# A recurrent layer's second-half products and output product taken from fp16 and bf16 parts

## The reference

```
y  = layer_norm(x)
xi = y @ w_ih.T + b_ih                       # 768 gates' inputs per token
for each token:                              # 512 steps, one after the other
    r = sigmoid(xi_r + h @ w_hr.T + b_hr)    # h: 256 numbers for each sequence
    z = sigmoid(xi_z + h @ w_hz.T + b_hz)
    n = tanh(xi_n + r * (h @ w_hn.T + b_hn))
    h = (1 - z) * n + z * h
x  = x + norm(norm(x) + h @ w_out.T + b_out)         # "first sum"
xf = norm(x)
e  = argmax(xf @ gate_W.T + gate_b)                  # one of 8 experts per token
m  = relu(xf @ wi_W.T + wi_b + (xf @ lora_A[e].T) @ lora_B[e].T)   # 512 hidden
x  = x + norm(m @ wo_W.T + wo_b)                     # "second sum"
```

## Time and profile before

| | |
|---|---|
| median of 3 runs | 1976.41 us (1976.2 to 1980.02) |
| the profiled execution | 1975.0 us |
| its span, first to last instruction | 1973.1 us |
| TensorE busy, products | 1683.9 us (85%) |
| VectorE busy | 1177.6 us (60%) |
| ScalarE busy | 739.8 us (37%) |
| first block, ahead of the recurrence | 0 to 33.9 us |
| its two writes of `Y1` and of `Y2`, 512 elements each | 2.6 us each (L361, L436) |
| `HS` from `HR` by DMA | 128 times 32 KB, 1.7 us from issue to landing |

### The profile page before, as it was taken

How to read it: one execution, slowest core, us unless ns; L and a number is a source line. 1 busy time by engine, 2 the same in 40 slices (tenths; PEclk the granted TensorE clock), 3 DMA queues, 4 the chain that set the end, 5 groups by cost and what they waited for, 6 DMA issues and landing times. The chain is left out here.

```text
span 1973.1 us, 68602 instructions
## 1 busy us (share of the span) xinstructions
PE 1683.9 (85%) x27122; PEld 1261.1 (64%) x27137; DVE 1177.6 (60%) x5580; ACT 739.8 (37%) x2556; POOL 362.9 (18%) x597
## 2 busy tenths in 40 slices
PE   4888878999999999999999988348988889897857
PEld 3676767888888888888888866224545455444423
DVE  5666666665655665556556544436676566675366
ACT  2333332222222222222222222014665566665645
POOL 2010100000000000000000012362123313411244
PEclk9999999999999999999999999977999899998979
DMA  5000000000000000000000000076436625732001
GB/s 121 7 8 7 7 7 7 5 3 4 3 5 5 4 4 3 4 3 4 3 4 3 4 1 0 2 118 99 60 54 91 99 25 79 101 56 28 1 6 38
DMA packets 80562, 53.56 MB, mean 27 GB/s; under 512 B 28558, under 2 KB 80166, under 8 KB 80422
## 3 DMA queue, kind: packets, MB, share of 16 engines
q1 hardware_dynamic: 78566, 51.54, 16.5%
q10 hardware_dynamic: 1856, 0.07, 0.1%
HBM read 31.84 MB, written 15.47 MB: 24 GB/s over the span
## 5 line engine op out<-in xcount | busy, mean ns | idle before, releaser
L653 PEld LDWEIGHTS PS<-G,W 128*128 128x128 f16 x18432 | 548.4, 105 | 181.2 <-DVE G L896 164.4
L653 PE MATMUL PS<-G,W 128*128 128x8 f16 x18432 | 577.7, 168 | 89.3 <-DVE G L896 85.5
L1700 DVE TENSOR_REDUCE MX<-PS 128x1 f32<-128x512 f32 (+3 forms) x352 | 223.0, 636 | 191.9 <-PE PS L1447 182.5
L805 ACT ACTIVATE tr<-PS 128x16 f32<-128x16 f32 x512 | 96.3, 188 | 578.3 <-PE PS L653 578.3
L1603 ACT ACTIVATE PT<-PS 128x512 f32<-128x512 f32 (+1 forms) x352 | 193.8, 559 | 171.0 <-PE PS L1463 167.1
L882 DVE SCALAR_TENSOR_TENSOR u_<-tr,PS 128x16 f32<-128x16 f32 x512 | 89.1, 174 | 274.7 <-PE PS L653 253.5
L666 PE MATMUL PS<-Y,V 128*128 (+1 forms) x2322 | 175.3, 192 | 0.0
L807 ACT ACTIVATE tz<-PS 128x16 f32<-128x16 f32 x512 | 93.7, 183 | 189.9 <-PE PS L653 189.9
L1444 PE MATMUL PS<-KS,QS 99*128 99x256 bf16 (+3 forms) x512 | 136.6, 319 | 31.6 <-DMA KS<-k_parts 20.7
L615 POOL TENSOR_TENSOR rt<-mv,eps 128x1 f32<-128x1 f32 x96 | 18.2, 189 | 746.9 <-DVE mv L917 746.9
L661 PE MATMUL PS<-ones,brow 3*128 3x32 bf16 x1032 | 141.0, 195 | 4.8 <-PEq L185 3.9
(11 more groups left out here) (324 smaller groups left out, 2677.4 us busy)
## 6 DMA issues: line engine op xcount, KB each, us to landing
QS<-q_parts SPq DMA_DIRECT2D x48, 256.0 KB
KS<-k_parts SPq DMA_DIRECT2D x48, 256.0 KB
q_parts<-PQ SPq DMA_DIRECT2D x16, 384.0 KB, 12.8
k_parts<-PK SPq DMA_DIRECT2D x16, 384.0 KB, 13.1
HS<-HR SPq DMA_DIRECT2D x128, 32.0 KB, 1.7
X<-in_L_attn_x_dram SPq DMA_DIRECT2D x4, 512.0 KB, 8.8
out_dram<-X SPq DMA_DIRECT2D x8, 256.0 KB, 2.3
s_hh<-in_L_attn_w_hh_dram SPq DMA_DIRECT2D x1, 768.0 KB, 5.5
```

Of the source, the lines that this page charges most:

```text
L653: return pe.matmul(bank[:, p, o:o + B], W[:, kc, w:w + P], G[:, kc, :], start=False, stop=True, skip_group_check=True)
L805: act.activation(tr[:, :], pR[:, p, o:o + NSTEP], ACT.Tanh, scale=gate_scale).then_inc(hn_tr.sem, 1)
L1700: dve.tensor_reduce(MX[:, g % 2, heads[0]:heads[-1] + 1, NT - 1 - it], p_x[:, k % 2, 0:len(heads) * w].rearrange("p (a w) -> p a w", w=w), ...
```

## The change

- All fp32 products of the units become sums of products of 16-bit parts. `w_out`, the gate weights, `wi` and `wo` are scaled by powers of two and split into high and low fp16 (`OU`, `GA`, `WI`, `DN`) during the preparation of sequences 3 to 6. `p_gy`, `p_ga`, the `wi` product and `p_dn` are three fp16 products each (`TERMS`) where one fp32 product was.
- `lora_B` is split into three bf16 parts; `LB` holds four of them stacked on 128 rows and `LB2` two on 64 rows. The masked `ML` is split and repeated in `MP` (two operations at s = 15, two in the next unit's s = 0), turned by two bf16 transposes (s = 1) and copied to `LAT` and `LAT2` (s = 2). The bias of the hidden layer is a 3-row product `wibr`.
- `p_base` takes one whole PSUM bank; per chunk it is one 3-row product, three 128-row products, one 128-row product with `LB` and one 64-row product with `LB2`. Chunks 0 and 1 are made at s = 3, chunks 2 and 3 at s = 4. One relu of 512 elements (s = 5) writes the high part `IH`; VectorE makes the low part `IL` in two halves of 256 (s = 6, 7); `p_dn` follows at s = 8 and 9, `T2` at 10, moments at 11 and 12, `N2` and the sum at 14.
- `XFT` becomes `XH` (ScalarE) and `XL` (VectorE), both at s = 11.
- The states are stored as parts: `GB` replaces `G1` and `G2`, the DMA copies `GB` to an fp16 `HS`, `HB` is two copies of 256 elements. `HR` stays for the step. The wait for the DMA moves ahead of the high part's write.
- `Y1` and `Y2` have the token innermost. So the gates' values in PSUM lie in the order chunk, sequence, step: the 16 values of a step are 16 bytes apart, and each product writes 8 columns at that distance.

The diff, cut to its core:

```diff
-        Y1 = sb(gru_scope, "Y1", [P, S + U, B], FP16)
-        HS = sb(gru_scope, "HS", [P, S, HC, B])
+        Y1 = sb(gru_scope, "Y1", [P, B, S + U], FP16)
+        HS = sb(gru_scope, "HS", [P, S // U, 2, U, NSTEP], FP16)
...
+            GB = sb(ctx, "GB", [P, 2, 2, U, NSTEP], FP16)
...
-                        sp.dma_start(HS[:, bass.ds(at, U)]..., HR[:, p])
+                        sp.wait_ge(g2_ready.sem, ...)
+                        sp.dma_start(HS[:, bass.ds(sp.snap(q * 2 + p), 1)]..., GB[:, p])
...
-                    o = NSTEP * k + B * mc
-                    return pe.matmul(bank[:, p, o:o + B], W[:, kc, w:w + P], G[:, kc, :],
+                    at = mc * U * B
+                    state = GB[:, p, part, k - 1, :] if k else GB[:, 1 - p, part, U - 1, :]
+                    return pe.matmul(bank[:, p, at:at + U * B].rearrange("p (b u) -> p b u", u=U)[:, :, k], W[:, kc, w:w + P],
+                                     state[:, kc * B:(kc + 1) * B], ...)
...
-                                    pe.matmul(o, V[:, w], Y[:, rows, :].rearrange("p s b -> p (s b)"),
+                                    pe.matmul(o, V[:, w], Y[:, :, rows],
...
+                TERMS = ((0, 0), (0, 1), (1, 0))
...
+                    if s == 12:
+                        for h, w in TERMS:
+                            last = pe.matmul(p_ga, (XH, XL)[h][:, :], GA[w][:, :], ...)
...
+                    if s == 1:
+                        pe.wait_ge(mlp.sem, mlp.value(pe, u))
+                        pe.transpose(p_laT[:, 0:P], MP[:, 0:4, :]..., identb[:, :])
+                        pe.transpose(p_laT[0:2 * E * R, P:2 * P], MP[:, 4:6, :]..., identb[:, :])
+                    for c in {3: (0, 1), 4: (2, 3)}.get(s, ()):
+                        at, o = slice(c * P, (c + 1) * P), p_base[:, c * P:(c + 1) * P]
+                        pe.matmul(o, wibr[:, at], ones3w[:, :], start=(c == 0), ...)
+                        for h, w in TERMS:
+                            pe.matmul(o, WI[w][:, at], (XH, XL)[h][:, :], ...)
+                        pe.matmul(o, LB[:, at], LAT[:, :], ...)
+                        last = pe.matmul(o, LB2[:, at], LAT2[:, :], ...)
+                    for c in {8: (0, 1), 9: (2, 3)}.get(s, ()):
+                        for h, w in TERMS:
+                            last = pe.matmul(p_dn, (IH, IL)[h][:, c, :], DN[w][:, c, :], ...)
...
-                    act.activation(tr[:, :], pR[:, p, o:o + NSTEP], ACT.Tanh, scale=gate_scale).then_inc(hn_tr.sem, 1)
+                    now = lambda bank: bank[:, p, 0:U * NSTEP].rearrange("p (n u) -> p n u", u=U)[:, :, k]
+                    act.activation(tr[:, :], now(pR), ACT.Tanh, scale=gate_scale).then_inc(hn_tr.sem, 1)
...
-                        for c in range(HC):
-                            act.activation(HB[:, c, :], HS[:, rows, c, one].rearrange("p s o -> p (s o)"), ACT.Copy)
+                        for h in range(2):
+                            src = HS[:, rows, h, :, :].rearrange("p g u (c b) -> p c g u b", c=HC)[:, :, :, :, one]
+                            act.activation(HB[:, h, :, :].rearrange("p c (g u) -> p c g u", u=U), src..., ACT.Copy)
...
+                    if s == 5:
+                        act.activation(IH[:, :, :].rearrange("p c n -> p (c n)"), p_base, ACT.Relu)
...
-                    dve.scalar_tensor_tensor(flat(G1), zg[:, :], 0.5, zn[:, :], ALU.mult, ALU.subtract).then_inc(g1_ready.sem, 1)
                     if k == 0:
                         gone = first * 2 + 16
                         dve.wait_ge(hr_out[p].sem, gone if isinstance(first, int) else dve.snap(gone))
+                    high = GB[:, p, 0, k, :]
+                    dve.scalar_tensor_tensor(high, zg[:, :], 0.5, zn[:, :], ALU.mult, ALU.subtract).then_inc(g1_ready.sem, 1)
...
+                    if s == 11:
+                        dve.tensor_tensor(XL[:, :], p_xfT, XH[:, :], ALU.subtract).then_inc(xl.sem, 1)
+                    if s == 15:
+                        dve.tensor_copy(MP[:, 2:5, :], ML[:, :].unsqueeze(1).to_broadcast([P, 3, E * R]))
+                        dve.tensor_tensor(MR_[:, :], ML[:, :], MP[:, 2, :], ALU.subtract)
+                    if s == 0:
+                        dve.tensor_copy(MP[:, 0:2, :], MR_[:, :].unsqueeze(1).to_broadcast([P, 2, E * R]))
+                        dve.tensor_tensor(MP[:, 5, :], MR_[:, :], MP[:, 0, :], ALU.subtract)
+                    if s in (6, 7):
+                        c = slice(2 * (s - 6), 2 * (s - 5))
+                        dve.scalar_tensor_tensor(IL[:, c, :], p_base..., 0.0, IH[:, c, :], ALU.max, ALU.subtract)
...
-                        dve.tensor_tensor(Y2[:, P:S, q:q + 1]..., PS[:, 6, 0:3 * P], Y1[:, P:S, q:q + 1]..., ALU.subtract)
+                        dve.tensor_tensor(Y2[:, q, P:S], PS[:, 6, 0:3 * P], Y1[:, q, P:S], ALU.subtract)
...
+                    if q == 3 and s == 2:
+                        biggest(fmx[:, 2:3], flat3(woT))
+                    if q == 3 and s == 3:
+                        biggest(fmx[:, 3:4], wiT[:, :])
+                    if q == 5 and s == 1:
+                        low(WI[1][:, :], wiT[:, :], fS[:, 3:4], WI[0][:, :])
+                    if q == 5 and s == 3:
+                        low(flat3(DN[1]), flat3(woT), fS[:, 2:3], flat3(DN[0]))
```

More of the change, by code:

```diff
@@ L515, in build @@
             p_gy = PS[:, 6, 0:D]
+            p_dn = PS[:, 6, 0:D]
+            p_ga = PS[:, 6, 0:E + E * R]
             p_xfT = PS[:, 7, 0:P]
[L517 to L522, removed]
+            p_laT = PS[:, 7, 0:P].bitcast(BF16)
+            p_base = PS[:, 7, :]
+            hb = signal("hb_copied", 2)
             x0 = signal("x0_ready")
@@ new lines, in late @@
+                        if c == FC - 1:
+                            last.then_inc(base.sem, 1)
+                    for c in {8: (0, 1), 9: (2, 3)}.get(s, ()):
+                        if c % 2 == 0:
+                            pe.wait_ge(ilow.sem, ilow.value(pe, u, c // 2 + 1))
+                        if c == 0 and not (isinstance(u, int) and u == 0):
+                            pe.wait_ge(t2.sem, t2.before(pe, u))
+                        for h, w in TERMS:
+                            last = pe.matmul(p_dn, (IH, IL)[h][:, c, :], DN[w][:, c, :], start=(c == 0 and h == 0 and w == 0),
+                                             stop=(c == FC - 1 and h == 1), skip_group_check=True)
@@ L777, in prepare @@
                             last.then_inc(tail_ps.sem, 1)
+                    if q == 3 and s == 5:
+                        pe.wait_ge(fsc.sem, fsc.value(pe, 0, 8))
+                        pe.transpose(PS[0:6, 6, 3 * P:], fmx[:, :], ident[:, :]).then_inc(fps.sem, 1)
+                    if q == 3 and s == 12:
+                        pe.wait_ge(tail_low.sem, tail_low.value(pe, 0, 4))
+                        pe.transpose(PS[0:1, 6, 3 * P:3 * P + 6], fcol[:, :], ident[0:6, 0:6]).then_inc(fps.sem, 1)
+                    if q == 4 and s == 2:
+                        pe.wait_ge(fsc.sem, fsc.value(pe, 0, 14))
+                        pe.matmul(PS[:, 6, 3 * P:3 * P + 4], onesr[:, :], frow[:, 0:4], start=True, stop=True).then_inc(fps.sem, 1)
+                    if q == 6 and s == 8:
+                        pe.wait_ge(hv.sem, hv.value(pe, 0, 4))
+                        pe.wait_ge(fsc.sem, fsc.value(pe, 0, 22))
+                        rows = PS[0:3, 7, 2 * P:].bitcast(BF16)
+                        for c in range(FC):
+                            last = pe.transpose(rows[:, c * P:(c + 1) * P], wibp[:, c, :], identb[:, :])
+                        last.then_inc(fps.sem, 1)
                     if q == 6 and s == 6:
@@ L932, in early @@
                         dve.wait_ge(gy.sem, gy.value(dve, u))
-                        dve.tensor_tensor(T[:, :], X0b[:, :], p_gy, ALU.add).then_inc(t_sum.sem, 1)
+                        dve.scalar_tensor_tensor(T[:, :], p_gy, finv[:, 0:1], X0b[:, :], ALU.mult, ALU.add).then_inc(t_sum.sem, 1)
                     if s == 4:
@@ new lines, in prepare @@
+                    if q == 4 and s == 3:
+                        dve.wait_ge(fps.sem, fps.value(dve, 0, 3))
+                        dve.tensor_scalar(finv[:, 0:4], PS[:, 6, 3 * P:3 * P + 4], 2.0 ** -14, None, ALU.mult).then_inc(fsc.sem, 1)
+                    if q == 4 and s == 4:
+                        step(15)
+                        dve.reciprocal(fS[:, :], finv[:, 0:4]).then_inc(fsc.sem, 1)
+                        dve.tensor_tensor(finv[:, 4:5], finv[:, 2:3], finv[:, 3:4], ALU.mult).then_inc(fsc.sem, 1)
@@ new lines, in prepare @@
+                    if q == 6 and s == 3:
+                        step(20)
+                        dve.tensor_copy(wibp[:, :, 1], wibq[:, :]).then_inc(fsc.sem, 1)
+                    if q == 6 and s == 4:
+                        step(21)
+                        dve.tensor_tensor(wibp[:, :, 2], wibq[:, :], wibp[:, :, 1], ALU.subtract).then_inc(fsc.sem, 1)
+                    if q == 6 and s == 10:
```

(2 more changed lines are left out.)

316 lines of the change are left out of this document (227 added, 89 removed).

## The result

| | time, median (lowest to highest) | ratio to before, 95% interval | profiled execution: time, span |
|---|---|---|---|
| before | 1976.31 us (1971.65 to 1980.02) | | 1975.0, 1973.1 us |
| changed | 2003.93 us (1998.64 to 2007.79) | 1.0145 (1.0121 to 1.017) | 1998.64, 1996.8 us |

Forecast were 1965 us and a range of 1908 to 1998. The changed kernel is slower.

The account below looks back on a forecast made before the run. Steps have a 1.94 us chain as floor, and filler outlasting its gaps adds 4.5 us per unit. Terms 12 - 2 + 2.5 + 13 - 4 - 5 - 5 = 11.5 us won gave 1965 us, range 1908 to 1998.

Parts of the forecast that it names:

- The step that failed: Units' steps on TensorE: 16-bit products of 128 columns issue at 56 ns each, not the skill's 81.
- the forecast's own signs of being wrong: Prediction wrong if `base` isn't the costliest filler, or if VectorE's `IL` or `N2` holds more than 0.5.
- The forecast's 0.91, 1.22, 0.03 and 0.03: Units' steps 3, 4, 8 and 9: us by which filler exceeds TensorE's free 0.97 us per step.
- a last unit: Last eight units without steps: the chain takes over, 12.2 us each against 11.44 before; 5 us lost in all.
- 0.6 x 23: Units' steps: excess falls from 4.5 to 3.9 us per unit over 23 units, 13 us won.
- Changes of height: `base` on TensorE: each change of contraction height costs 0.11 us beside a load's pitch; three per chunk.
- the first rival: `base`: height changes overlap, 1.74 us less per unit and a shorter tail, 1913 us; chance 0.23.
- Strided operands of the step: Recurrence's PSUM operands 16 bytes apart: 0.01 us per step, 5 us lost; rival, every step longer, 1991 us at 0.06; chance 0.17.
- Preparation and start: `Y1`, `Y2` writes to neighbouring elements win 12 us, added splitting loses 2, the first block wins 2.5.
- The wait for the states' DMA: Ahead of the high part at every fourth step: only its issue counts, 0.03 x 128, 4 us lost.
- VectorE and ScalarE: Units' filler over free time: VectorE steps 0, 6, 14, 15 at 0.27, 0.40, 0.45, 0.30; ScalarE step 1 at 0.25 us.
- the third rival: `HB`'s strided fp16 read costs what the strided write does: 35 us more, 2000 us; chance 0.08.

Follow-up runs that it names:

- experiment 2: Changed kernel with the same 24 products of `base` in order of height, 4 changes of height per unit in place of 14: 1971.95 us, ratio 0.9994.
- experiment 1: Changed kernel with the bias rows behind the second LoRA operand's 64 rows, five full-height products per chunk of `base`: 1942.63 us, ratio 0.9848.
- the recurrence's half alone: Kernel before with `Y1` and `Y2` by sequence and gates' PSUM order half, sequence, step; second layer unchanged: 1963.60 us, ratio 0.9933.
- experiment 9: Changed kernel with bias folded, `dn` spread, `WI` products early, plus `X0` and `N1` moved and last units' output product first: 1888.69 us, ratio 0.9554.
- Experiment 3: Changed kernel with extra 512-column products, whose result nobody reads, in TensorE's waits of the last eight units: 2000.03 us, one run.

## Why the prediction was wrong

- *The step that failed* is "56 ns each ... the trace shows 56 at the full clock, and the sum goes by it". The row is of a stretch of the attention layer in which TensorE runs at 2.4 GHz; the price was needed in the scan, where it runs at 1.2. I took the reading 1.00 of the earlier trace rows for the level without holding it against a duration. The trace of the kernel before held the answer twice. Its `XF` transpose takes 461 ns in the units and its counterpart of the last layer 311. And 100 us ahead of the earlier trace rows, in the same layer, the clock reads 0.50, and the same kind of products takes 0.43 us for four, not 0.22:

```profile
1346.90:1348.30 1.40, 1.29 (x10) 1.01 (x11) 0.91 (x3) 0.00 (x0) 0.00 (x0) 0.50 0.45 135
```

```profile
1347.41 0.63 PE L1447 MATMUL PS<-maskU,identb 128*128 128x128 bf16 x4
1347.84 0.63 PE L1460 MATMUL PS<-QS,KS 102*128 102x512 bf16 x1
```

The other two pitches of the earlier trace rows, 28 ns for 8 and 32 columns, are too short to show it: a quarter of 107 is 27. None of the forecast's own signs of being wrong names this either. `base` was the costliest filler, as it says, and `IL` and `N2` held 0.25 and 0.36; what spoke were steps 3 and 4 at 3.50 and 3.66 for 2.9 and 3.2.
- *What it was worth.* Of the 42 products of 128 columns in a unit, 39 lie in steps that TensorE ends (15 in step 3, 12 in 4, 6 each in 8 and 9), each 0.051 us dearer: 2.0 us. The forecast's 0.91, 1.22, 0.03 and 0.03 become 1.68, 1.83, 0.34 and 0.34, measured 1.55, 1.71, 0.30 and 0.30. In a last unit 36 of them lie on the chain: 12.2 + 36 x 0.051 = 14.0, measured 13.9. 23 x 2.0 + 8 x 1.8 = some 60 us. The profiled execution is 35 us above the 1963.5 forecast for it; what gave back the rest are some 0.6 us per unit, half in these four steps and half in VectorE's and ScalarE's (14 us), the strides and the DMA wait (6), the unchanged rest (2), and about 3 that I can't assign. So other terms that were too dear hid part of the miss. (The forecast's sum has 13 for 0.6 x 23, which is 13.8.)
- *Changes of height* were right at 0.11 beside the pitch (0.11 in experiment 2, and 0.65 - 6 x 0.056 = 0.31 for three at the full level). That they overlap, the first rival, is refuted: ten of them less, with every product still there, are worth 1.09 us per unit. The 102-row products that spoke for it show no change beside 128 rows because they count as full height, as the 67 rows of experiment 1 do. The Trainium skill, TensorEngine Tiling (Array Packing), Key Properties, has a change of tiling mode drain the engine. The 0.11 us are in line with that, but no run shows the mode itself.
- *Strided operands of the step*, the rival that ended slower: 0.006 us per step, 3 us of the 5 taken. It would have needed 0.022. The Trainium skill, SBUF — State Buffer, Door 1: The DMA port swizzle, has non-contiguous PSUM patterns slow matmuls significantly; for 8 single elements per product the runs show next to nothing, while a scattered moving operand of 32 columns cost 0.03 per product.
- *Preparation and start*: 12.5 us forecast, 13.0 measured, and 14.0 in the recurrence's half alone (285.5 for 299.5), which has none of the added splitting. The writes were sized to 0.01 (472 and 550 ns for 0.47 and 0.55).
- *The wait for the states' DMA*: 4 us taken, nothing seen (steps with and without it are 1.94 to 1.95).
- *VectorE and ScalarE*: step 0 0.44 for 0.27 (the last operation on `MP` takes 0.44 us beside GpSimd's `X0b` and 0.19 without it, experiment 9), 1 0.05 for 0.25, 6 0.25 for 0.40, 14 0.36 for 0.45, 15 0.28 for 0.30. Together 0.3 us per unit less than forecast. `HB`'s read did not cost what the write does: the third rival falls.
- The Trainium skill, TensorE: Matmul & The Clock Gate, Wait — 56ns, not 53.3ns?, gives 106.7 ns at N = 128 for an array at 1.2 GHz and 55.6 at 2.4. Experiment 3 shows both, 0.107 and 0.056 to 0.06. I had weighed that page's 81 ns instead, which fits neither level here.

## What to carry to other kernels

Take a price from the stage in which it will be paid, and check the clock of a stage by a duration that depends on it (a long product, a transpose), not by the granted clock alone. Where TensorE is at half rate, narrow products hide it (0.027 us for 8 and for 32 columns in this scan) and wide ones pay in full, so a change from few fp32 to many 16-bit products should first give up every product and every change of height that another operand's spare rows can carry. Then lay filler in the steps that another engine ends: the same arithmetic went from 2004 to 1889 us that way.

## What the runs showed of the hardware

- The granted clock read 1.00 over the scan in four profiles (before, changed, experiments 1 and 9) and 0.50 in the other seven, with steps of the same length. In this scan the durations agree with 0.50 in all of them: experiment 1 reads 1.00, and its 128-column products follow each other at 0.107 us.
- Busy for 85 to 97% of the scan by the profile, in products of 8 to 384 columns, TensorE stayed at 1.2 GHz for all of it; with bursts of 512-column products in the waits of the last units it was at 2.4 GHz for part of the time.
- A VectorE operation of 32 columns with two inputs in SBUF takes 0.44 us while GpSimd adds two SBUF tiles (0.45 us), and 0.19 without that.
- A product whose moving operand has its 32 columns 1032 bytes apart takes 0.06 us for 0.03.
